# Batched bilinear scores in fp32: TensorE's program laid out in lines of 256 instructions with branch hints, and the tail matmuls over all 128 rows

## What is computed

```python
B, F, E = (512, 200, 64)
bilinear = jnp.einsum('bie,ied->bid', feature, weight)   # weight: (200, 64, 64)
out = jnp.einsum('bid,bjd->bij', bilinear, feature)      # (512, 200, 200)
```

## Time and profile before

| what | value |
|---|---|
| median of 3 runs | 347.33 us (344.71 to 351.31) |
| profiled execution | 347.19 us |
| its span, first to last instruction | 345.4 us |
| mean granted TensorE clock | 0.93 of full speed |
| TensorE matmuls and weight loads | 7296 each |

### The profile page before, as it was taken

The page is one execution under the profiler, slowest core; times in us unless marked ns, Lnnn a source line. Parts: engine busy times, 40 slices in busy tenths (PEclk is TensorE's granted clock), DMA queues, the critical chain, the costliest instruction groups (busy, mean ns, idle before and its releaser), DMA issues.

```text
span 345.4 us, 15674 instructions
## 1 busy us (share of the span) xinstructions
PE 250.5 (73%) x7296; PEld 221.2 (64%) x7296; DVE 148.4 (43%) x172; ACT 128.3 (37%) x177; POOL 2.4 (1%) x5
## 2 busy tenths in 40 slices
PE   0167679599967674969785967869985877987870
PEld 0156668378867573748775957748875766766760
DVE  0042455136634541605563553504653554635550
ACT  1032426045524422314452443403553444442540
POOL 2000000000000000000000000000000000000000
PEclk9987899899989988989998798989999999999995
DMA  7999998847999997757799999964899997746796
GB/s 302 423 426 423 400 368 280 331 193 289 351 409 399 395 388 261 236 242 291 300 374 418 395 366 421 306 286 194 335 373 390 407 386 312 289 199 260 284 408 286
DMA packets 21808, 115.70 MB, mean 335 GB/s; under 512 B 2416, under 2 KB 2416, under 8 KB 21360
## 3 DMA queue, kind: packets, MB, share of 16 engines
q1 hardware_dynamic: 21744, 114.70, 84.6%
HBM read 32.77 MB, written 81.92 MB: 332 GB/s over the span
## 4 chain that ended last, share of the span: by engine, by line
PE 72%; issue 19%; DMA 4%; DVE 1%; SPq 1%; ACT 1%
PE psum L238 46%; PE psum L210 16%; PE psum L255 9%; DMA w_sb<-w_dram 4%; PE psum L222 1%; DVE tile L270 1%; SPq L128 1%; ACT mixed L291 1%
## 5 line engine op out<-in xcount | busy, mean ns | idle before, releaser
L238 PE MATMUL psum<-x_sb,mixed 64*64 64x200 f32 x3072 | 173.2, 357 | 32.9 <-issue 29.5
L238 PEld LDWEIGHTS psum<-x_sb,mixed 64*64 64x64 f32 x3072 | 141.4, 143 | 49.5 <-issue 41.2
L270 DVE COPY tile<-psum 128x800 f32<-128x800 f32 x100 | 99.2, 992 | 141.2 <-PE psum L238 128.9
L270 ACT COPY tile<-psum 128x800 f32<-128x800 f32 x100 | 82.7, 827 | 117.2 <-PE psum L238 85.5
L210 PE MATMUL psum<-x_sb,w_sb 64*64 64x64 f32 x3072 | 67.7, 228 | 37.3 <-issue 21.3
L210 PEld LDWEIGHTS psum<-x_sb,w_sb 64*64 64x64 f32 x3072 | 65.6, 140 | 40.6 <-issue 39.5
L291 DVE COPY mixed<-psum 64x512 f32<-64x512 f32 x48 | 33.1, 689 | 28.2 <-PE psum L210 26.9
L291 ACT COPY mixed<-psum 64x512 f32<-64x512 f32 x48 | 27.9, 581 | 43.6 <-PE psum L210 43.0
L255 PE MATMUL psum<-x_sb,tails 64*32 64x200 f32 x1024 | 32.6, 377 | 13.0 <-issue 13.0
L255 PEld LDWEIGHTS psum<-x_sb,tails 64*32 64x32 f32 x1024 | 22.6, 115 | 21.7 <-issue 18.3
L293 ACT COPY mixed<-psum 128x512 f32<-128x512 f32 x24 | 14.1, 587 | 44.3 <-PE psum L210 44.2
## 6 DMA issues: line engine op xcount, KB each, us to landing
out_dram<-tile SPq DMA_DIRECT2D x96, 800.0 KB, 6.3
x_sb<-x_dram SPq DMA_DIRECT2D x16, 800.0 KB, 8.7
x_sb<-x_dram SPq DMA_DIRECT2D x32, 400.0 KB, 7.7
w_sb<-w_dram SPq DMA_DIRECT2D x2, 2048.0 KB, 16.7
out_tail_dram<-tile SPq DMA_DIRECT2D x4, 800.0 KB, 4.5
w_sb<-w_dram SPq DMA_DIRECT2D x1, 2304.0 KB, 22.5
```

Of the source, the lines that this page charges most:

```text
L238: last = nc.tensor.matmul(psum[half_rows(pair), n % BANK_PAIRS * 2 + h, a * FIELDS:(a + 1) * FIELDS], mixed[half_rows(h), (CHUNKS * g + c) ...
L270: copy(tile[:, k % SLOTS, engine], psum[:, bank:bank + 2, 0:2 * FIELDS]).then_inc(copied[engine], 1)
```

## The change

TensorE's program is cut into blocks called lines. `Lines.take` is told before each unit and each matmul how many instruction slots come, and counts them. When the count would pass 244, it ends the line with a branch to the next one, pads to a multiple of 256 slots (the padding is branched over) and begins the next with a branch hint that names the branch at that line's end and its target. A branch leads from the common start to line 0, and one from the last line to the end.

The tail uses all 128 rows. `tails` becomes, for each quad, two blocks of 32 columns, one for each sample of the pair; in a block 16 columns are used, 8 for half 0 and 8 for half 1, and the 8 of one half are zero in the partitions of the other. One call thus gives the tail rows of a sample of each half, and two calls are accumulated into a place instead of four: 32 calls per tail unit instead of 64. The tail mix's result is copied half by ScalarE and half by VectorE. The host's reordering of the tail follows.

```diff
@@ -93,7 +93,7 @@
         add(n, 1 if m % 2 == 0 else 2, 2 if m % 2 == 0 else 1, "mix", g, c, m)
 
     def tail_mix(n, g):
-        add(n, 1, 0, "tail_mix", g)
+        add(n, 1, 1, "tail_mix", g)
 
     walk(score, tail, mix, tail_mix)
     return copies, number, tiles
@@ -101,6 +101,37 @@
 
 COPIES, NUMBER, OUT_TILES = count_copies()
 TILE_OF = {tile: k for k, tile in enumerate(OUT_TILES)}
+
+
+class Lines:
+
+
+
+    SIZE, MATMUL, WAITS, ROOM = 256, 4, 3, 244
+
+    def __init__(self, nc, pe):
+        self.nc, self.pe, self.count = nc, pe, 0
+        pe.br("pe_line0")
+        self.begin()
+
+    def begin(self):
+        name = f"pe_line{self.count}"
+        self.pe.addr_align(self.SIZE, 0, 0)
+        self.nc.switch_bb(name)
+        self.hint = self.pe.mark_branch_hint_location()
+        self.used = 1
+        self.count += 1
+
+    def take(self, size):
+
+        if self.used + size > self.ROOM:
+            self.pe.br(f"pe_line{self.count}").branch_hint(self.hint)
+            self.begin()
+        self.used += size
+
+    def end(self):
+        self.pe.br("pe_end").branch_hint(self.hint)
+        self.nc.switch_bb("pe_end")
 
 
 def build(nc, x, weight, out, out_tail):
@@ -109,7 +140,8 @@
     x_sb = sb("x_sb", [128, 3, QUADS, PART, 2])
     mixed = sb("mixed", [128, 2, QUADS, CHUNK, 2])
 
-    tails = sb("tails", [128, HALF_SAMPLES // 4, 4, TAIL_TILE + TAIL])
+
+    tails = sb("tails", [128, QUADS, 2 * TAIL_TILE // (2 * TAIL), HALVES, TAIL])
     tile = sb("tile", [128, SLOTS, 2, HALVES, 2 * FIELDS])
     psum = nc.alloc_psum_tensor("psum", [128, 2 * BANK_PAIRS, BANK], F32)
 
@@ -169,6 +201,8 @@
 
         @block.tensor
         def _(pe):
+            lines = Lines(nc, pe)
+
             def wait_banks(n):
 
                 if n >= BANK_PAIRS:
@@ -195,6 +229,7 @@
                 return x_sb[half_rows(h), g % 2:g % 2 + 2, quad, :, pair]
 
             def mix(n, g, c, m):
+                lines.take(lines.WAITS)
                 wait_banks(n)
                 wait_part0(g)
                 pe.wait_ge(w_loaded[c], 16)
@@ -207,18 +242,21 @@
                     for swap in range(2):
                         field = first + swap * BANK_FIELDS + r
                         for h in range(HALVES):
+                            lines.take(lines.MATMUL)
                             last = nc.tensor.matmul(
                                 psum[half_rows(h ^ swap), bank + swap, r * HALF_SAMPLES:(r + 1) * HALF_SAMPLES],
                                 w_sb[half_rows(h), field, :], x_field(g, h, field), start=True, stop=True)
                 last.then_inc(unit_ready, 1)
 
             def tail_mix(n, g):
+                lines.take(lines.WAITS)
                 wait_banks(n)
                 pe.wait_ge(w_loaded[CHUNKS - 1], 16)
                 for p in range(PIECES):
                     wait_part1(g, p)
                 for r in range(TAIL):
                     for h in range(HALVES):
+                        lines.take(lines.MATMUL)
                         last = nc.tensor.matmul(
                             psum[half_rows(h), n % BANK_PAIRS * 2, r * HALF_SAMPLES:(r + 1) * HALF_SAMPLES],
                             w_sb[half_rows(h), TAIL_FIRST + r, :], x_field(g, h, TAIL_FIRST + r),
@@ -242,24 +282,27 @@
                 last.then_inc(unit_ready, 1)
 
             def tail(n, g, e):
+                lines.take(lines.WAITS)
                 wait_banks(n)
                 if e == 0:
                     pe.wait_ge(zeroed, 1)
                     wait_copies(NUMBER["tail_mix", g])
-                for piece in range(2):
-                    for b in range(4):
-                        for tile4 in range(4):
-                            four = 8 * e + 4 * piece + tile4
-                            for h in range(HALVES):
-                                weights = tails[half_rows(h), four].rearrange("p b w -> p (b w)")
+                for half_unit in range(2):
+                    for piece in range(2):
+                        for pair in range(2):
+                            for column in range(4):
+                                quad = 16 * e + 8 * half_unit + 4 * piece + column
+                                weights = tails[:, quad].rearrange("p b h r -> p (b h r)")
+                                lines.take(lines.MATMUL)
                                 last = nc.tensor.matmul(
-                                    psum[tile4 * TAIL_TILE:(tile4 + 1) * TAIL_TILE, n % BANK_PAIRS * 2 + h,
-                                         piece * FIELDS:(piece + 1) * FIELDS],
-                                    weights[:, b * TAIL_TILE:(b + 1) * TAIL_TILE],
-                                    x_sample(g, h, 2 * four + b // 2, b % 2), start=b == 0, stop=b == 3)
+                                    psum[column * TAIL_TILE:(column + 1) * TAIL_TILE,
+                                         n % BANK_PAIRS * 2 + half_unit, piece * FIELDS:(piece + 1) * FIELDS],
+                                    weights[:, pair * TAIL_TILE:(pair + 1) * TAIL_TILE],
+                                    x_sb[:, g % 2:g % 2 + 2, quad, :, pair], start=pair == 0, stop=pair == 1)
                 last.then_inc(unit_ready, 1)
 
             walk(score, tail, mix, tail_mix)
+            lines.end()
 
         def copies(eng, copy, engine):
 
@@ -293,11 +336,11 @@
                     copy(to, source).then_inc(copied[engine], 1)
 
             def tail_mix(n, g):
-                if engine == 0:
-                    eng.wait_ge(unit_ready, n + 1)
-                    eng.wait_ge(zeroed, 1)
-                    source = psum[:, n % BANK_PAIRS * 2, :].rearrange("p (r f b) -> p f b r", r=TAIL, b=4)
-                    copy(tails[:, :, :, 0:TAIL], source).then_inc(copied[engine], 1)
+                eng.wait_ge(unit_ready, n + 1)
+                eng.wait_ge(zeroed, 1)
+                source = psum[half_rows(engine), n % BANK_PAIRS * 2, :].rearrange(
+                    "p (r q b) -> p q b r", r=TAIL, q=QUADS)
+                copy(tails[half_rows(engine), :, 0:4:3, engine, :], source).then_inc(copied[engine], 1)
 
             walk(score, tail, mix, tail_mix)
 
@@ -334,8 +377,8 @@
     rows = r["out_dram"].reshape(GROUPS, CHUNKS, TILES, 2, CHUNK, 2, HALVES, 2, FIELDS)
     rows = rows.transpose(0, 6, 2, 5, 7, 3, 1, 4, 8).reshape(GROUPS, HALVES, HALF_SAMPLES, TAIL_FIRST, FIELDS)
 
-    tail = r["out_tail_dram"].reshape(GROUPS, 4, 4, TAIL, 2, HALVES, 2, FIELDS)
-    tail = tail.transpose(0, 5, 4, 6, 1, 2, 3, 7).reshape(GROUPS, HALVES, HALF_SAMPLES, TAIL, FIELDS)
+    tail = r["out_tail_dram"].reshape(GROUPS, 4, 2, HALVES, TAIL, 2, 2, 2, FIELDS)
+    tail = tail.transpose(0, 3, 5, 6, 7, 1, 2, 4, 8).reshape(GROUPS, HALVES, HALF_SAMPLES, TAIL, FIELDS)
     whole = np.concatenate([rows, tail], axis=3)
 
     whole[1::2] = np.concatenate([whole[1::2, ..., PART:], whole[1::2, ..., :PART]], axis=-1)
```

## The result

The changed kernel takes 398.14 us (median of 4 runs, 396.17 to 399.18), the kernel before beside it 347.79 us (4 runs, 344.71 to 351.31): ratio 1.1475, 95% interval 1.1381 to 1.1569. The forecast was 351 us, the range 302 to 364. The profiled execution took 396.17 us for a span of 394.3 us.

A forecast was written before the change was run, and what follows sets the result against it. TensorE waiting for its program, fetched one 256-instruction line at a time, was taken as the bound. 23.8 + 302.8 + 12.3 + 11.1 = 350.0 us of span, plus 1.8, less 1 for corrections: 351 us; range 302 to 364.

The forecast's parts named there:

- What bounds the kernel: TensorE's pauses, 63.8 us in all, are waits for its program, fetched 256 instructions a packet, one in flight.
- about 4.6 us: Claimed time to bring TensorE's next line of 256 instructions; about 6 us under full DMA load.
- Stepping through the order of work with that rule gives 60 lines: TensorE's program, closed before 244 slots, was to fill 60 lines, most of 114 matmuls, against 125.7 before.
- The hint has nothing to bring forward: At each line's start: the next line is fetched at entry anyway, so hint and branch cost nothing; chance 0.40.
- the sum: Span of the whole run: 23.8 us start, 302.8 for 55 lines, 12.3 last matmuls, 11.1 end, together 350.0 us.
- Rival 1: The hint puts a second line in flight, pauses go and DMA bounds: 307 us; chance 0.33, full or in part.
- Rival 2: Each line's branch adds its length between arrival and use, 0.20 us: 362 us; 0.27 shared with rival 3 and extreme.
- Its extreme: A branch drops the fetch under way, a line takes 4.2 + 4.6 us, the run about 530 us; 3 in 100.
- Rival 3: Tail's 128-row weight loads don't overlap with matmuls: 6 us more, 357 us; 0.27 shared with rival 2 and its extreme.
- The tail: Tail units: 64 matmuls replace 128, 48 ns each, again 3.0 us a unit; halved in instructions, not in time.
- the prediction's correction: The four lines' worth of tail matmuls removed were cheap, 4.5 to 5 us each: up to 3 us more.
- the correction that I had set at up to 4 us: Lines with 11 fewer matmuls get shorter where TensorE was the longer one: up to 4 us less over a dozen.

The follow-up runs named there:

- the tail alone: The changed kernel's 128-row tail without lines, hints or branches: 333.96 us, ratio 0.9679 to the kernel before; measured again on another chip, 336.45 us, ratio 0.9792.
- the aligned kernel: The changed kernel with padding ahead of each branch, so each line begins on a multiple of 256 slots: 338.12 us, ratio 0.9831 to the kernel before.
- the two shifted kernels: Lines padded to start on multiples of 256 slots, then moved by 128 or 224 slots, branch at slot 127 or 223: 409.68 us and 549.46 us.
- the lines alone: The kernel before, old tail kept, with the changed kernel's unpadded lines, hints and branches added: 414.94 us, ratio 1.2112 to the kernel before.

## Why the prediction was wrong

- *What bounds the kernel:* right. TensorE waits for its own program, 256 instructions a packet, one in flight; every experiment's time follows the packets and their distance, and no kernel shows a second one in flight, with hints two blocks ahead either. But "about 4.6 us" for a line is no floor: in the kernel before packets come as close as 3.4 us (from 155.7 to 159.1 us), around a tail unit.
- *"Stepping through the order of work with that rule gives 60 lines":* wrong for the kernel that ran. I read the padding off the source. The built program keeps none, and so 53 packets, and branches that drift through the blocks. This was needed for the loss: in the layout as drawn the branch leads into the next block, and the hint costs nothing.
- *"The hint has nothing to bring forward ... I take its cost and the branch's at nothing":* the step that failed. The reason given for it, that the sequential fetch starts at entry, holds only while no hint is pending whose branch leads back into the same block. Where one is, the packet waits for the branch: 4.29 us behind entry where it was 3.25, and the matmuls ahead of the branch lie on the path. 52 x 6.84 = 355.7 us stand where the sum had 55 x 5.505 = 302.8.
- *The bounds of that step* were -63.8 us and +4.6 us a line. The measured cost, by the medians of the tail alone (334.0 us) and the changed kernel (398.1 us), is 64 us in 52 blocks, 1.2 us each, inside these bounds (by the ratios, which take out the chips, 62 us); I took the value at the end where nothing happens, and let the range end at 364 us because the rival that I priced for "slower" was another mechanism.
- *Rival 1 (a second line in flight):* not seen in any kernel. *Rival 2 (the branch between arrival and use):* a branch with its hint costs 0.12 us and not 0.20, and explains 7 us of 64. Its extreme, 4.2 + 4.6 us a line, is by its arithmetic close to what moving the branch to slot 223 gives (8.82 us), but that is chance: no fetch is dropped there (59 packets), it is sent late. *Rival 3 (128-row weight loads):* wrong. A tail unit of the aligned kernel takes what one took before, 3.03 us for its 64 matmuls, 47 ns apart as forecast. Its 64 weight loads of 108 ns would fill 6.9 us one after another, so they run beside matmuls although all use the same rows:

```profile
148.62 3.03 PE psum L298 x60
```

- *The tail:* the instructions are halved and the time of a unit is not, as said. But the blocks that went are not worth the mean price of 5.505 us, nor the 4.5 to 5 us of the prediction's correction: four packets less brought 7 to 11 us by the two ratios, not 22, since they came out of the stretches with tail matmuls, where packets were as little as 3.4 us apart.
- *The padded layout, had it run:* 338.1 us against my 351, or 342 by its ratio to the kernel before. A block of 114 matmuls cost 5.17 us, not 5.505; the correction that I had set at up to 4 us was 10 to 14.

## What to carry to other kernels

Where TensorE's pauses come at a fixed count of instructions, the program is the bottleneck: count packets before costing anything else, and look for fewer instructions. Check from the packets and the spacing of pauses that a layout exists in the program that ran, not only in its source. A branch hint that is pending while branch and target lie in the block where execution already is cost the more the further into the block the branch stood; so put hinted branches at the very end of a block, set the hint directly ahead of its branch, or use no hint.

## What the runs showed of the hardware

- With a hinted branch pending whose target is in the block just entered, the packet of the next block comes only behind the branch: 4.01 and 6.44 us from entry to packet with the branch at slots 127 and 223, against 2.88 us with it at slot 255 and its target in the next block.
- The held-back packet starts 1.0 us behind the branch at the least (1.1 and 1.2 us in the two shifted kernels), in the median 2.3 to 2.4 us. A branch record lasts about 0.18 us where its target is there already. At the end of a filled block it lasts until the next block is there, up to 4.82 us.
- From a packet's start to the first instruction of its block 2.3 to 2.5 us pass in the median, of which about 0.95 us are the transfer. In the kernel before, a block's entry and the next packet lie 3.25 us apart on average where the block had been waited for, and 1.1 us at the least. The windows of 4.6 us in the earlier trace rows are 2.2 us of the one and 2.4 of the other, and no floor. What makes a fetch without a hint wait so differently is open.
- In no trace did TensorE hold a block more than the present and the next: with hints that named one further on, each block still began 2.4 us behind its own packet.
- The Trainium skill ("Runtime: NRT & Kernel Launch", section Instruction fetch mechanics) warns of branches whose target lies outside the two blocks present. The changed kernel's branches lead one instruction on, into the same block or the next, and as that rule has it none forces a fetch of its own: 53 packets bring the program once. The delay that they cause all the same, 21% of the time by the lines alone, is another thing, and shown by the runs here.
